# First cross attention with the probabilities stationary in split f32r, row sums from columns of ones, and powers of one key tile a step

## The reference

```python
kv = jnp.concatenate([y_main @ Wk + bk, y_main @ Wv + bv], axis=-1)
kv = kv.reshape(b, s2, H, 2 * HD)
k = _ln(kv[..., :HD], kn_w, kn_b)
v = kv[..., HD:]
ctx = _attn(qT, k.transpose(0, 2, 1, 3), v.transpose(0, 2, 1, 3))
ctx_dca = _attn(qT, k_dca.transpose(0, 2, 1, 3), v_dca.transpose(0, 2, 1, 3))
return (ctx + DCA_WEIGHT * ctx_dca) @ Wo + bo
```

## Time and profile before

| | |
|---|---|
| median of 3 runs | 2759.47 us (2752.17 to 2764.41) |
| profiled execution | 2750.2 us, span 2747.5 us |
| granted PE clock, mean | 0.939 |
| PE busy | 2434.7 us (89%) |
| PE weight loads | 2003.8 us (73%) |
| DVE busy | 1719.2 us (63%) |
| ACT busy | 1155.4 us (42%) |
| POOL busy | 1002.0 us (36%) |

### The profile page before, as it was taken

The page is one execution under the profiler, slowest core; times in us unless marked ns, Lnnn a source line. Parts: engine busy times, 40 slices in busy tenths (PEclk is TensorE's granted clock), DMA queues, the critical chain, the costliest instruction groups (busy, mean ns, idle before and its releaser), DMA issues. The chain is left out here.

```text
span 2747.5 us, 40047 instructions
## 1 busy us (share of the span) xinstructions
PE 2434.7 (89%) x12756; PEld 2003.8 (73%) x12756; DVE 1719.2 (63%) x2728; ACT 1155.4 (42%) x2084; POOL 1002.0 (36%) x688
## 2 busy tenths in 40 slices
PE   4699999999999969998898899999999997788744
PEld 2588888888888748886676678888888876566632
DVE  3457766766767723333443278888788884666677
ACT  1344444443444313332221367666676662332211
POOL 3147667667667610000011035544555460110000
PEclk9699999999999979998899899999999999899957
DMA  3000000000000012210231200000000002110010
GB/s 103 1 25 25 25 1 25 25 1 25 19 7 1 1 64 69 68 61 17 68 86 37 83 25 25 16 18 17 26 25 16 10 1 76 52 41 31 12 62 16
DMA packets 104256, 89.51 MB, mean 33 GB/s; under 512 B 32752, under 2 KB 82432, under 8 KB 104080
## 3 DMA queue, kind: packets, MB, share of 16 engines
q1 hardware_dynamic: 103792, 87.28, 10.5%
q0 software_dynamic: 288, 0.00, 0.0%
HBM read 86.22 MB, written 1.05 MB: 32 GB/s over the span
## 5 line engine op out<-in xcount | busy, mean ns | idle before, releaser
L2184 POOL TENSOR_TENSOR xT<-xT,x1b_ring 128x512 f32<-128x512 f32 (+1 forms) x176 | 248.3, 1411 | 213.4 <-ACT x1b_ring L2314 206.7
L869 POOL TENSOR_TENSOR x0b_krstd<-x0b_krstd,minus_half 128x24 f32<-128x24 f32 x64 | 267.0, 4173 | 108.7 <-DVE x0b_krstd L933 87.9
L889 POOL TENSOR_TENSOR xT<-xT,x0b_ring 128x512 f32<-128x512 f32 (+1 forms) x176 | 243.8, 1385 | 142.4 <-ACT x0b_ring L1078 130.6
L983 DVE TENSOR_TENSOR x0b_ring<-x_ps,x0b_krstd 128x512 f32<-128x512 f32 (+1 forms) x208 | 143.0, 688 | 134.4 <-PE x_ps L828 132.2
L111 DVE TENSOR_TENSOR x1b_plo<-x1b_ring,x1b_phi 128x512 fp32r<-128x512 f32 (+1 forms) x208 | 222.2, 1068 | 6.6 <-issue 4.9
L854 PE MATMUL x_ps<-x0b_ring,x0b_vn 128*128 128x256 f32 (+1 forms) x832 | 217.5, 386 | 1.8 <-ACT x0b_ring L1078 1.6
L828 PE MATMUL x_ps<-x0b_qbd,x0b_kT 128*128 128x256 f32 (+1 forms) x832 | 217.6, 384 | 1.6 <-DVE x0b_ring L983 1.4
L1078 ACT ACTIVATE x0b_ring<-x0b_ring 128x512 f32<-128x512 f32 (+1 forms) x208 | 130.7, 630 | 207.7 <-DVE x0b_ring L961 197.3
L2329 ACT ACTIVATE x1b_ring<-x_ps,x1b_keymask 128x512 f32<-128x512 f32 (+1 forms) x208 | 143.1, 688 | 131.3 <-DVE xT L2256 126.0
L116 PE MATMUL x_ps<-x1b_qy,x1b_yT 128*128 128x512 f32 (+1 forms) x416 | 175.8, 423 | 4.3 <-ACT x1b_ring L2329 2.9
L828 PEld LDWEIGHTS x_ps<-x0b_qbd,x0b_kT 128*128 128x128 f32 (+1 forms) x832 | 149.9, 187 | 30.1 <-issue 6.4
(11 more groups left out here) (575 smaller groups left out, 5844.5 us busy)
## 6 DMA issues: line engine op xcount, KB each, us to landing
x_y<-in_ctx_dram SPq DMA_DIRECT2D x8, 1536.0 KB
x_y<-in_ctx_dram SPq DMA_DIRECT2D x24, 512.0 KB, 3.8
a_wn<-in_L_attn_W_Q_dram SPq DMA_DIRECT2D x16, 256.0 KB, 3.1
a_wn<-in_L_attn_W_K_dram SPq DMA_DIRECT2D x16, 256.0 KB, 3.5
a_wn<-in_L_attn_W_V_dram SPq DMA_DIRECT2D x16, 256.0 KB, 4.1
a_won<-in_L_attn_W_O_dram SPq DMA_DIRECT2D x16, 256.0 KB, 2.9
x1a_wq<-in_L_xattn_Wq_dram SPq DMA_DIRECT2D x4, 1024.0 KB, 10.7
x1c_wo<-in_L_xattn_Wo_dram SPq DMA_DIRECT2D x8, 512.0 KB, 6.9
```

Source lines behind the costliest of these rows:

```text
L869: ins = g_.tensor_tensor(r, r, c.minus_half[:, 0:8].unsqueeze(1).broadcast_to([P, whole, 8]), ALU.pow)
L889: g_.tensor_tensor(total[half][0:m, :], old, src, ALU.add).then_inc(summed, 1)
L983: v.tensor_tensor(slot.rearrange("p (h s) -> p h s", s=S), ps[0:m, S_BANK + n % 2, :].rearrange("p (h s) -> p h s", s=S), spread(krstd[0:m ...
L2184: g_.tensor_tensor(total[half][0:m, :], old, src, ALU.add).then_inc(summed, 1)
```

## The change

- The product is turned round. The probabilities of two heads (128 columns: 2 heads x 64 tokens) are stationary, and the values of these two heads move. Both are split in f32r. `vn` holds for each key tile and pair of heads 64 high values, 2 ones, and 64 low values. The high probabilities multiply all 130 columns, the low ones the first 66, so the columns of ones give the row sums. Four pairs a tile: 8 matmuls in place of 2.
- ACT copies the high part of the probabilities (one step behind the exponential), POOL makes the low part, where it added the row sums. There are 4 buffers for high parts and 2 for low ones.
- The values: ACT copies the high part, DVE now splits off the low part, and only then is the bank free.
- The flips and spreads of row sums go. DVE inverts the row sums, adds the two halves of the product and multiplies; PE transposes the result back (entries T, in steps 5 and 18 of the next sequence, in a projection bank), and DVE adds it to the context.
- POOL takes powers of one key tile a step, 6 steps ahead of the tile's scores.
- The flip of the maxima uses the score bank that is idle, and the projection banks are 5 to 7 in place of 3, 5 and 6. Several small tensors lie in space of `c.xn` and `c.xT`, and the last sequence has 20 steps of tail in place of 18.

```diff
+        VD = 2 * HD0
+        VW = VD + 2
+        vn = st.sb("vn", [P, KT, H0 // 2, VW + VD], F32R)
+        p_high = [st.sb(f"phi{i}", [P, COLS], F32R) for i in range(4)]
+        p_low = [st.sb(f"plo{i}", [P, COLS], F32R) for i in range(2)]
+        PAST = entries("5:T0 18:T1")
+        LAST = entries("31:T0 44:T1")
+        STEPS = TILES + 20
...
+                    if kind == "T":
+                        pe.wait_ge(normed, 3 * (2 * seq + e[2]) + 3)
+                        for g in range(2):
+
+                            mm = pe.transpose(out[:, g * P:(g + 1) * P], onew[:, 2 * g:2 * g + 2, :].rearrange("p k n -> p (k n)"), c.ident[:, :])
...
-                    f = half_at(part, n, 28)
-                    if f is not None:
-
-                        pe.wait_ge(summed, (KT - 1) * (2 * seq + f + 1))
-                        pe.wait_ge(rowmax_done, 3 * (2 * B if part == "last" and f == 1 else 2 * seq + f + 2))
-                        for t in range(4):
-                            mm = pe.transpose(ps[:, X_BANK, t * P:(t + 1) * P], total[f % 2][:, t * P:(t + 1) * P], c.ident[:, :])
-                        mm.then_inc(sum_flipped, 1)
-                    f = half_at(part, n, 29)
-                    if f is not None:
-                        pe.wait_ge(rowsum_done, 2 * (2 * seq + f) + 2)
-                        for t in range(4):
-                            mm = pe.transpose(ps[:, X_BANK, t * P:(t + 1) * P],
-                                              inverse[:, f % 2, t:t + 1].broadcast_to([P, P]), c.ident[:, :])
-                        mm.then_inc(sum_spread, 1)
...
-                        pe.wait_ge(exp_done, TILES * seq + (t + 1))
+                        pe.wait_ge(p_done, TILES * seq + (t + 1))
...
-                        for g in range(2):
-                            mm = pe.matmul(ps[:, O_BANK, g * GC:(g + 1) * GC], vn[0:m, kt, half, g * P:(g + 1) * P],
-                                           ring[0:m, key_slot(par, t, LIFE), g * GC:(g + 1) * GC],
-                                           start=(kt == 0 and g == 0), stop=(kt == KT - 1), skip_group_check=True)
+                        for i in range(4):
+                            hi, lo = (a[0:m, i * P:(i + 1) * P] for a in (p_high[(t + TILES * par) % 4], p_low[t % 2]))
+                            col = (i % 2) * (VW + VD)
+                            values = vn[0:m, kt, 4 * half + i, :]
+                            pe.matmul(ps[:, O_BANK + i // 2, col:col + VW + VD], hi, values,
+                                      start=(kt == 0 and i % 2 == 0), stop=False, skip_group_check=True)
+                            mm = pe.matmul(ps[:, O_BANK + i // 2, col:col + VW], lo, values[:, 0:VW],
+                                           start=False, stop=(kt == KT - 1), skip_group_check=True)
...
+                def deviation(seq, n):
+
+                    half, kt = n // KT, n % KT
+                    if kt in (0, 3, 6, 9):
+                        g_.wait_ge(w_done, 8 * seq + (4 * half + kt // 3 + 1))
+                        g_.sem_inc(apart, 1)
+                    r = krstd[0:size(kt), half, kt, :]
+                    g_.tensor_tensor(r, r, c.minus_half[0:size(kt), 0:8], ALU.pow).then_inc(rstd_done, 1)
...
+                        if not (part == "first" and t < 2):
+                            g_.wait_ge(pv_done, TILES * seq + (t - 1))
+                        g_.wait_ge(p_hi, TILES * seq + (t + 1))
+                        g_.sem_inc(apart, 1)
+                        split(g_, p_high[(t + TILES * par) % 4][0:m, :], p_low[t % 2][0:m, :],
+                              ring[0:m, key_slot(par, t, LIFE), :]).then_inc(p_done, 1)
...
+                    if e[1] == "V":
+                        _, _, kt = e
+                        m = size(kt)
+                        v.wait_ge(v_hi, KT * seq + (kt + 1))
+                        split(v, vn[0:m, kt, :, 0:VD], vn[0:m, kt, :, VW:VW + VD],
+                              ps[0:m, bank, :].rearrange("p (h d) -> p h d", d=VD)).then_inc(v_done, 1)
+                        v.wait_ge(v_done, KT * seq + (kt + 1))
+                        v.sem_inc(kv_free[bank], 1)
...
+                        v.reciprocal(inverse[:, :], osb[:, :, VD]).then_inc(normed, 1)
+                        v.tensor_tensor(onew[:, :, :], osb[:, :, 0:VD], osb[:, :, VW:VW + VD], ALU.add).then_inc(normed, 1)
+                        v.wait_ge(normed, 3 * (2 * seq + f) + 2)
+                        v.tensor_tensor(onew[:, :, :], onew[:, :, :], spread(inverse[:, :], VD), ALU.mult).then_inc(normed, 1)
...
+                    t = lagged(part, n, LAG_HI)
+                    if t is not None:
+                        m = size(t % KT)
+                        if not (part == "first" and t < 4):
+                            act.wait_ge(pv_done, TILES * seq + (t - 3))
+                        act.wait_ge(exp_done, TILES * seq + (t + 1))
+                        act.activation(p_high[(t + TILES * par) % 4][0:m, :], ring[0:m, key_slot(par, t, LIFE), :], ACT.Copy
+                                       ).then_inc(p_hi, 1)
```

More of the change, by code:

```diff
@@ L675, in x0_main_attention @@
                         "22:K020 23:K021 24:W02 24:Y30 25:Y31")
+        PAST = entries("5:T0 18:T1")
+        LAST = entries("31:T0 44:T1")
+        STEPS = TILES + 20
         def made_at(part, n):
+            past = [] if part == "first" else PAST.get(n, [])
+            here = HERE.get(n, []) + (LAST.get(n, []) if part == "last" else [])
             ahead = [] if part == "last" else AHEAD.get(n, [])
-            return [(0, e) for e in HERE.get(n, [])] + [(1, e) for e in ahead]
+            return [(-1, e) for e in past] + [(0, e) for e in here] + [(1, e) for e in ahead]
         BEFORE = [(1, *e) for n in sorted(AHEAD) for e in AHEAD[n]]
@@ L719, in steps @@
                         step("body", ("body", i, rel), 2 * i + (1 + rel), 1 - rel, n)
-            for n in range(TILES + 18):
+            for n in range(STEPS):
                 step("last", ("last", ITERATIONS, 0), B - 1, (B - 1) % 2, n)
@@ L894, in _ @@
-                steps(g_, lambda e: deviations(0, e[2], e[3]) if e[1] == "W" else None, step)
+                def deviation(seq, n):
[5 more added lines that the diff above has]
+                    g_.tensor_tensor(r, r, c.minus_half[0:size(kt), 0:8], ALU.pow).then_inc(rstd_done, 1)
@@ L896, in _ @@
+                for n in range(RSTD_AHEAD):
+                    deviation(0, n)
+                steps(g_, lambda e: None, step)
             @block.vector
@@ L926, in take @@
                         v.wait_ge(y_done, 8 * seq + (2 * q + ch + 1))
+                        v.sem_inc(kv_free[bank], 1)
[6 more added lines that the diff above has]
+                        v.wait_ge(v_done, KT * seq + (kt + 1))
+                        v.sem_inc(kv_free[bank], 1)
+                    if e[1] == "T":
+                        _, _, f = e
+                        v.wait_ge(kv_full[bank], nth + 1)
+                        v.sem_inc(apart, 1)
+                        for j in range(4):
+                            rows = slice(32 * j, 32 * j + 32)
+                            o = ctxT[rows, 2 * f:2 * f + 2, bass.ds(seq * S, S)]
+                            new = ps[rows, bank, 0:2 * P].rearrange("p (g h n) -> p g h n", g=2, h=2)[:, :, j % 2, :]
+                            ins = v.tensor_tensor(o, new, o, ALU.add)
+                        ins.then_inc(added, 1)
+                        v.wait_ge(added, 2 * seq + (f + 1))
                         v.sem_inc(kv_free[bank], 1)
```

115 lines of the change are left out of this document (39 added, 76 removed).

## The result

The changed kernel takes **2787.6 us** (median; 2773.5 to 2792.8), the kernel before 2755.3 in all its runs: a ratio of **1.0095, 95% interval 1.0068 to 1.0123**. The forecast was 2747 with a range of 2725 to 2850; the time is in the range, on the slower side. The time was expected to fall by 0.45% and rose by 0.95%. The profiled run took 2787.6 us (span 2785.5), against 2750.2 (span 2747.5) before. The changed kernel's runs fall into two groups, three near 2774 and four near 2789, and its median lies in the upper one. The ratio goes by all runs and says some 26 us; the two profiled spans differ by 38 us, since the profiled run is one of the upper group.

The account below looks back on a forecast made before the run. PE was taken as the bound, 96% busy at 2.4 GHz. From 2750.2: 3 (product), 10.4 (transposes) and 7 (waits and tail) off, 8 (couplings) on, giving 2737.8; with 9.3 from profiled run to median, 2747 us, range 2725 to 2850.

Parts of the forecast that it names:

- the sentence that gave the clock no chance: PE in the stage: a lower clock from more waiting for loads got no chance of its own; clock stays 0.98 and 0.99.
- C: Product loop, every product: a short f32r column costs as in f32, product 1.33 us, 99 us slower, 2846; chance 0.19.
- E: POOL bounds the light steps, from 3.25 us a step; 35 us in all, 2782; chance 0.16.
- The product: PE, per key tile: 8 weight loads of 107 ns, 0.856 us against 0.87, 3 us gained over 208 steps.
- B: Product loop: 17 ns of an f32r matmul come on top of each load, 28 us, 2775; chance 0.13.
- D: Product loop: f32r loads faster than the slope says, product 0.46 us, 82 us less before POOL's share, 2683; chance 0.06.
- the 10.4 us: PE: sum flips and inverse spreads go, 32 transposes come; 96 x 0.108 us gained.
- The 21.4 us: PE's wait for the row maxima in the whole stage, forecast to stay.
- my 8 us: Small couplings of DVE, ACT and PE: 8 us lost, estimated as 1 us a sequence, bounds 0 and 25.
- 632 us forecast: POOL: 208 splits at 1.40 us and 208 powers at 1.64, 3.04 us a step, hidden but tight.
- ACT and DVE: ACT gains 131 us of copies, DVE 72 us of value splits, which fit in its 112.5 us waiting for scores.
- Signs: Forecast marks: product matmuls 107 ns apart, PE busy 95% or more, POOL about 632 us, PE never waiting for the split.

Follow-up runs that it names:

- the filled variance sums: The changed kernel with the variance sums' 4 columns repeated to 64: 2759.3 us, ratio 1.0026.
- the first experiment: The changed kernel, but the low part of the probabilities multiplies all 130 columns of the values instead of 66: 2758.4 us, ratio 1.001.
- the turned f32 kernel: The changed kernel without the split: product turned round in plain f32, 4 matmuls of 66 columns a tile, POOL only taking powers: 2747.2 us, ratio 0.9975.
- The kernel with a short product of its own: The kernel before with four f32 matmuls of 64 columns a tile instead of two of 256, half the product left out: 2760.6 us, ratio 1.0017.

## Why the prediction was wrong

**The step that failed** is the sentence that gave the clock no chance: "the variance sums are pure loads already and the clock stays at 0.98 and 0.99". The row was read rightly and the inference was false. The kernel before had stretches of pure loads between products that streamed almost without a pause; the change makes the products such stretches too, so that in the light steps one follows the other. What held for 1.6 us of loads between full matmuls didn't hold for both together. It cost some 63 us of PE time, half of the 140 - 15 us that PE was busy at 1.2 GHz. About 18 of these were hidden, because PE stood idle 15 us and no longer 33. The wide low part and the filled variance sums give back 29 and 28 us of median, 23 and 19 by the ratios. That 2787.6 us still lies in the range is luck: its upper part was there for C, which did not happen, and E's 2782 is close by chance.

**The product, mis-sized by a little.** Forecast 0.856 us against 0.87, 3 us gained. That the loads set its price and the columns don't was right, and at 2.4 GHz the pairs come 0.223 us apart (the median), so B (2 x 124 = 0.25 us), C (0.33) and D (0.12) are excluded. But that is 112 ns a load and not 107. The 107 was an average over 16 variance sums, four of which are of the key tile of 49, with shorter loads; between the sums of full tiles the trace of the kernel before has 112 ns too. Eight loads are then 0.893 us, 0.031 more than the old product. This is what the traces show from start to start: a product with the scores behind it, up to the variance sums, takes 1.725 us before and 1.756 in the changed kernel (medians from 200 to 900 us). How the 1.756 is shared varies with the columns, 0.81 and 0.95 in the changed kernel and 0.84 and 0.91 with the wide low part. The kernel before with only its product made short has 1.755 and the turned product in plain f32 1.756, so it goes with the eight loads, in f32 and f32r alike. 208 x 0.031 = 6 us **lost** instead of 3 gained. The Trainium skill (TensorE: Matmul & The Clock Gate, LDWEIGHTS) puts a load at P/1.2 ns, 107 ns for 128; the measured 112 ns at the higher level are 5% above it. At the lower level the pair takes 0.43 us, twice as long, so what it says comes near at 2.4 GHz only.

**Transposes, idle time, tail.** The groups of sum flips and spreads are gone and 32 transposes came, so the 10.4 us hold by count; I didn't test them alone. PE's wait for the last sum is gone. The 21.4 us of waiting for the maxima were to stay; they fell to 5.9 while PE ran slower and to 12.8 in the first experiment, and in both the couplings, my 8 us, are small: 3.0, 2.8 and 2.7 us for L793, L842 and the split in the changed kernel, 4.8, 2.7 and 2.7 in the first experiment. Idle time in all fell, by 18 and 7 us. **The sum made again** for the kernel with the wide low part, whose PE is busy 13.6 us more than before: clock (49 - 15)/2 = 17, product and scores 6, transposes -10.4, 13 together. Its idle time is 6.5 us less, its stage 6 us longer, and its ratio 1.001 (0.999 to 1.003). So with most of the clock back the change is worth nothing that can be told, where I had 12 us.

**POOL, right.** 632 us forecast, 360.3 + 273.6 = 634 measured. A power of 8 elements took 1.73 instead of 1.64 and a split 1.32 instead of 1.40: 3.05 us a step for 3.04, and hidden. That POOL can decide was shown on the kernel before with powers one tile a step, at 3.27 us in a step and 23 us slower; the point of 3.25 us was not tested in the changed kernel. What I didn't see is that spreading the powers is itself worth 11 to 25 us beside splits; I had counted the 4.17 us block only as an argument against E. The Trainium skill (SBUF — State Buffer, two separate sides) has a GpSimd operation that reads SBUF and a VectorE operation with two SBUF inputs exclude each other. A power took 1.90 us beside the adds, 1.73 here, 1.65 in the turned f32 kernel, where POOL has nothing else in the stage, and 1.64 in the rows of before; DVE's running maximum runs in all of them and no run took it away, so none shows whether the lock is the reason.

**ACT and DVE, right in kind.** DVE's wait for the scores fell from 112.5 to 51.7 us, and it is busy 568 - 534 = 34 us more, where I had 72. ACT has 109 us more (441 - 332; forecast 131), and neither holds PE.

**Signs.** The distance of the pairs (within 5%), the POOL groups and the idle time under 40 us came as the forecast's signs had it, and yet the time was wrong. One of them misled. I had written that PE should be busy 95% or more, as a mark of the forecast. It is busy 99%, and that is the fault: at half the clock the same work keeps PE busy for longer and hides its pauses. The busy share confirms nothing without the granted clock beside it.

What stays open: the mechanism by which the clock is granted. The runs show which programs lose it and that columns behind loads bring it back; they don't show by what measure. The kernel with a short product of its own kept the clock between scores and sums and stayed at 1.2 GHz in its tail, and the changed kernel with still fewer columns lost no more. Nor was the faster group of the changed kernel's runs, near 2774 us, profiled; that they spend less time at the lower level is my guess.

## What to carry to other kernels

Where weight loads set the pace of a product, as here with 66 to 130 columns a load, splitting f32 into f32r parts buys nothing, since the eight loads cost the same (1.756 us with the scores, either way); turn the product in f32 and save the splitting. Before shortening the matmuls behind the loads, look at what stands next to them: loads after loads with few columns can halve the clock, though PE is never idle, and the granted clock has to be read stretch by stretch after such a change. If it has fallen, useless columns behind the loads can bring it back: here they cost nothing in the product, at most 0.14 us in a group of variance sums (1.74 us against 1.60 up to the next product), and brought back 19 to 29 us.

## What the hardware showed that I had not expected

- Adding 64 columns to half of the product's matmuls, or 60 to each variance sum, made this kernel 0.7 to 1% faster; taking 64 away from the other half of the product's changed nothing that could be told.
- The clock fell to 1.2 GHz in stretches with PE busy 10.00 of 10.00 and 9.00 of 9.00 us, within a product that followed variance sums.
- Twelve load-bound products in a row, 20 us, ran at 1.2 GHz (0.51 over the 33 us around them), with PE busy throughout, after a pause at which the clock had fallen.
- At the lower level the loads slow down as well: a pair of load-bound matmuls went from 0.22 to 0.43 us and a product from 0.90 to 1.57.
- A power of 8 elements a partition on GpSimd took 1.64 to 1.90 us on average, by what else the kernel ran.
